# Unread matmuls ahead of two stretches of a transformer kernel, and its step lists reordered

## What is computed

```python
x = x + ln(phazor_conv(ln(x)))        # decaying complex filter along the tokens, real part
x = x + ln(moe8_top2(ln(x)))          # 8 experts of width 64, top 2, and a shared expert of 128
x = x + ln(attention(ln(x)))          # 16 heads of 64, l2-normed q and k, alibi, causal, 2 null keys
x = x + ln(moe4_top2(ln(x)))          # 4 unlike experts: swiglu 512, folded MLP, a two-norm block, MLP 512
```

## Time and profile before

| | before |
|---|---|
| median of the three runs | 1136.36 us |
| the profiled execution | 1135.25 us |
| its span, first to last instruction | 1133.5 us |
| PE / DVE / POOL / ACT busy | 90 / 69 / 51 / 49 % of the span |
| mean granted TensorE clock | 0.963 of full speed |

### The profile page before, as it was taken

The page is one execution under the profiler, slowest core; times in us unless marked ns, Lnnn a source line. Parts: engine busy times, 40 slices in busy tenths (PEclk is TensorE's granted clock), DMA queues, the critical chain, the costliest instruction groups (busy, mean ns, idle before and its releaser), DMA issues.

```text
span 1133.5 us, 18951 instructions
## 1 busy us (share of the span) xinstructions
...
## 2 busy tenths in 40 slices
...
DMA packets 21869, 11.29 MB, mean 10 GB/s; under 512 B 7440, under 2 KB 21136, under 8 KB 21648
## 3 DMA queue, kind: packets, MB, share of 16 engines
...
## 4 chain that ended last, share of the span: by engine, by line
PE 55%; DVE 24%; POOL 11%; issue 7%; ACT 2%; ACTq 0%; DVEq 0%; POOLq 0%
PE bank L1839 10%; POOL rnorm L835 7%; PE bank L1615 7%; PE bank L1841 4%; PE bank L1608 4%; PE bank L1609 3%; PE bank L1610 3%; PE bank L1739 3%; PE bank L1959 3%; PE bank L1965 3%; PE bank L1918 2%; PE bank L1799 2%; DVE sumsq L1435 2%; PE bank L1805 1%; PE bank L1869 1%
## 5 line engine op out<-in xcount | busy, mean ns | idle before, releaser
L835 POOL TENSOR_TENSOR rnorm<-sumsq,minus_half 128x16 f32<-128x16 f32 x64 | 187.7, 2949 | 21.6 <-DVE sumsq L1438 21.4
L843 POOL TENSOR_TENSOR unit<-unit,causal 128x256 f32<-128x256 f32 x128 | 89.7, 732 | 109.0 <-ACT unit L1062 109.0
L843 POOL TENSOR_TENSOR square<-square,causal 128x256 f32<-128x256 f32 x128 | 90.5, 737 | 101.4 <-ACT square L1062 101.4
L1799 PE MATMUL bank<-qT,kT 64*128 64x256 f32 x512 | 96.6, 389 | 0.0
L1462 DVE TENSOR_TENSOR denom<-bank,null_sum 128x4 f32<-128x4 f32 x128 | 20.3, 158 | 105.5 <-PE bank L1841 105.5
L1068 ACT ACTIVATE qT<-bank 128x512 f32<-128x512 f32 x64 | 38.4, 601 | 109.7 <-PE bank L1615 109.6
L1444 DVE TENSOR_TENSOR unit<-unit,rnorm 128x1024 f32<-128x1024 f32 x64 | 78.9, 1240 | 12.6 <-POOL rnorm L835 12.4
L1615 PEld LDWEIGHTS bank<-ident,unit 128*128 128x128 f32 x520 | 62.8, 150 | 33.3 <-issue 15.5
L1435 DVE TENSOR_REDUCE sumsq<-square 128x16 f32<-128x1024 f32 x64 | 77.7, 1214 | 11.6 <-ACT square L1024 11.3
L1615 PE MATMUL bank<-ident,unit 128*128 128x128 f32 x520 | 73.3, 289 | 13.5 <-DVE unit L1444 10.2
L1839 PE MATMUL bank<-val,unit 128*128 128x128 f32 x512 | 81.7, 282 | 4.2 <-DVE mixed L1466 4.0
...
## 6 DMA issues: line engine op xcount, KB each, us to landing
...
```

The source lines that it names most:

```text
L835: pool.tensor_tensor(rnorm[:, k, t, :], sumsq[:, t % 2, k, :], minus_half[:], ALU.pow).then_inc(a_root.sem, 1)
L843: m = pool.tensor_tensor(pd, pd, causal[:].unsqueeze(1).to_broadcast([P, 2, P]), ALU.mult)
L1799: return mm(bank[s][:, 2 * P * b:2 * P * (b + 1)], kT[rs, c, 2 * P * b:2 * P * b + P], qT[rs, c, 2 * P * b:2 * P * (b + 1)], start=True, s ...
```

## The change

Twenty matmuls are added in the set-up in four lots of five (`s_warm.0` to `s_warm.3`) and sixteen ahead of the last group's `f_turn`, in two lots of eight (`f_warm.0`, `f_warm.1`). Each multiplies 128x128 by 128x512 of weights that are in place and writes bank 6; nobody reads that result, and the next step that uses the bank writes over it. Three of the set-up lots and one of the last wait for a count of norm steps. Three of them stand between `s_turn` and `l_turn3`, and one between `l_turn3` and `l_route`.

All lists of all four engines are reordered. None loses or gains another step.

```diff
 PROLOGUE = {
     "PE": """
-e_turn1 l_turn2 s_turn l_turn3 l_route s_fold1 l_g.0 s_fold2 l_cT l_u.0 s_fold3 l_c.0 s_fold4 l_g.1 l_c.1 l_u.1
+e_turn1 l_turn2 s_turn s_warm.0 s_warm.1 s_warm.2 l_turn3 s_warm.3 l_route l_g.0 s_fold1 s_fold2 l_cT l_u.0 s_fold3
+l_c.0 s_fold4 l_g.1 l_u.1 l_g.2 l_c.1 l_u.2 l_g.3 l_u.3 l_c.2 l_g.4 l_u.4 l_c.3 E_turn1 l_down.0 l_down.1 l_down.2
...
     "DVE": """
-s_phase s_gain e_stats s_shift s_decay e_apply s_conv s_last e_scan e_sum s_w0 l_turn2 s_scale l_res s_raw l_norm
-l_turn3 s_pad l_route l_pick l_coef l_hg.0 s_v2 l_cT E_stats s_kvlo l_hu.0 l_hc.0 E_apply s_bias l_hg.1 l_hu.1 s_qlo
+e_stats s_phase s_gain s_shift s_decay e_apply s_conv s_last s_w0 e_scan e_sum l_turn2 s_scale s_raw l_res l_norm
+l_turn3 l_route s_pad l_pick s_v2 l_coef l_cT E_stats l_hg.0 s_kvlo l_hu.0 l_hc.0 E_apply s_bias l_hg.1 s_qlo l_hu.1
...
     "POOL": """
-e_stats s_sel s_slopes e_scan s_fill l_turn2 s_scale l_res s_colb E_stats E_scan l_dstats.0 l_dstats.1 l_astats.0
+e_stats s_sel s_slopes e_scan s_fill s_scale l_turn2 s_colb l_res E_stats E_scan l_dstats.0 l_dstats.1 l_astats.0
...
 FIRST = {
     "DVE": """
-a_mix.15 l_dstats.0 l_end.0 l_dstats.1 l_astats.0 l_end.1 l_aapply.0 l_xl.0 l_astats.1 a_o.0 e_sum l_aapply.1 a_o.1
-a_end.0 a_end.1 l_xl.1
+l_hc.1 a_mix.7 l_hu.2 a_mix.8 a_mix.9 l_hc.2 a_mix.10 l_hu.3 a_mix.11 l_hg.4 a_mix.12 l_hc.3 l_hu.4 e_sum a_mix.13
+a_mix.14 a_mix.15 l_dstats.0 l_dstats.1 l_end.0 l_astats.0 l_end.1 l_aapply.0 l_astats.1 l_xl.0 a_o.0 l_aapply.1
...
 MIDDLE = {
     "DVE": """
-f_out.3 a_mix.0 f_end_stats e_stats a_mix.1 l_hu.0 l_coef l_hg.1 a_mix.2 e_apply a_mix.3 l_hu.1 e_scan a_mix.4
-l_hg.2 l_cT l_hc.0 a_mix.5 l_hu.2 a_mix.6 l_hc.1 a_mix.7 l_hg.3 a_mix.8 a_mix.9 a_mix.10 l_hu.3 f_end a_mix.11
-l_hc.2 l_hg.4 a_mix.12 l_hu.4 l_hc.3 a_mix.13 e_sum a_mix.14 l_dstats.0 a_mix.15 l_end.0 l_dstats.1 l_astats.0
-l_aapply.0 l_end.1 l_astats.1 a_o.0 a_end.0 l_aapply.1 l_xl.0 a_o.1 l_xl.1 a_end.1
+l_coef f_out.3 a_mix.0 f_end_stats l_hu.0 a_mix.1 l_hg.1 e_stats a_mix.2 e_apply a_mix.3 e_scan l_hu.1 a_mix.4 l_cT
+l_hg.2 a_mix.5 a_mix.6 l_hc.0 l_hc.1 a_mix.7 l_hu.2 a_mix.8 l_hg.3 l_hc.2 a_mix.9 a_mix.10 l_hu.3 a_mix.11 l_hc.3
+l_hg.4 a_mix.12 l_hu.4 a_mix.13 e_sum a_mix.14 f_end a_mix.15 l_dstats.0 l_end.0 l_dstats.1 l_astats.0 l_aapply.0
+l_end.1 l_xl.0 l_astats.1 a_o.0 l_aapply.1 a_end.0 a_o.1 l_xl.1 a_end.1
     "POOL": """
-f_stats.0 f_stats.1 a_ss.0.0 a_ss.0.1 f_ce a_ss.1.0 a_keep f_ce_apply a_ss.1.1 a_ss.2.0 a_ss.2.1 f_ce2 l_turn2
-a_ss.3.0 a_ss.3.1 l_res f_bias a_scores.0 a_scores.1 e_stats a_scores.2 a_scores.3 a_scores.4 e_scan a_scores.5
-f_end_stats a_scores.6 a_scores.7 l_dstats.0 l_dstats.1 l_astats.0 l_astats.1 a_o.0 a_o.1
+f_stats.0 f_stats.1 a_ss.0.0 a_ss.0.1 f_ce a_ss.1.0 a_ss.1.1 f_ce_apply a_ss.2.0 a_ss.2.1 f_ce2 l_turn2 a_ss.3.0
+a_ss.3.1 l_res f_bias a_scores.0 a_scores.1 e_stats f_end_stats a_scores.2 a_keep a_scores.3 a_scores.4 e_scan
+a_scores.5 a_scores.6 a_scores.7 l_dstats.0 l_astats.0 l_dstats.1 l_astats.1 a_o.0 a_o.1
...
 LAST_A = {
     "DVE": """
-a_o.0 a_o.1 a_end.0 a_end.1
+a_mix.15 a_o.0 a_end.0 a_o.1 a_end.1
...
 LAST_F = {
     "PE": """
-f_turn.0 f_turn.1 f_ce.0 f_ce.1 f_sw.0 f_me.0 f_me.1 f_sw.1 f_ml.0 f_ml.1 f_ceT f_sw.2 f_relu.0 f_ml.2 f_relu.1
+f_warm.0 f_warm.1 f_turn.0 f_turn.1 f_ce.0 f_ce.1 f_me.0 f_me.1 f_sw.0 f_ml.0 f_sw.1 f_ceT f_ml.1 f_sw.2 f_relu.0
...
+            def warm(count, w):
+
+                for _ in range(count):
+                    mm(bank[6][:], w[:, 0:P], w[:, 0:N], start=True, stop=True)
+
+            def s_warm(k):
+                if k == 0:
+                    pe.wait_ge(w0_rounded, 2)
+                    pe.wait_ge(n_y.steps.sem, n_y.steps.at(0, 9))
+                elif k == 1:
+                    pe.wait_ge(n_y.steps.sem, n_y.steps.at(0, 13))
+                elif k == 2:
+                    pe.wait_ge(n_l.steps.sem, n_l.steps.at(0, 9))
+                warm(5, w0_gate.hi)
+
+            def f_warm(g, k):
+                if k:
+                    pe.wait_ge(n_o.steps[1].sem, n_o.steps[1].at(g, 5))
+                warm(8, w_kv.hi)
```

More of the change, by code:

```diff
@@ L58 @@
     "PE": """
[L59 to L63, removed]
+a_m.0 a_m.1 a_null a_t.0 a_m.2 a_v.0 l_turn2 a_t.1 a_m.3 a_v.1 a_t.2 l_turn3 a_t.3 a_v.2 a_v.3 l_g.0 a_scores.0
@@ L67 @@
[L67 to L71 removed]
+a_ss.0.0 a_ss.0.1 a_u.0.0 a_ss.1.0 a_null a_u.0.1 a_ss.1.1 a_u.1.0 a_ss.2.0 a_u.1.1 a_ss.2.1 a_u.2.0 l_turn2
@@ L72 @@
+a_ss.3.0 l_res a_ss.3.1 a_u.2.1 l_norm a_u.3.0 a_u.3.1 l_turn3 a_nexp l_hg.0 l_route l_pick l_hu.0 a_mix.0 l_coef
+e_stats a_mix.1 l_hg.1 a_mix.2 e_apply l_hg.2 a_mix.3 e_scan a_mix.4 l_hu.1 l_cT a_mix.5 l_hc.0 l_hg.3 a_mix.6
+l_hc.1 a_mix.7 l_hu.2 a_mix.8 a_mix.9 l_hc.2 a_mix.10 l_hu.3 a_mix.11 l_hg.4 a_mix.12 l_hc.3 l_hu.4 e_sum a_mix.13
+a_mix.14 a_mix.15 l_dstats.0 l_dstats.1 l_end.0 l_astats.0 l_end.1 l_aapply.0 l_astats.1 l_xl.0 a_o.0 l_aapply.1
+a_o.1 a_end.0 l_xl.1 a_end.1
 """,
     "ACT": """
-a_m.0 a_m.1 a_t.0 a_m.2 a_v.0 a_t.1 a_m.3 a_v.1 a_t.2 l_turn3 a_t.3 a_nexp a_v.2 a_v.3 l_g.0 a_scores.0 a_scores.1
@@ L107 @@
-a_nexp l_g.0 a_scores.1 l_g.1 l_g.2 a_scores.2 a_oT.0 a_scores.3 l_cT a_scores.4 a_oT.1 a_oT.2 l_g.3 a_scores.5
-a_scores.6 a_oT.3 l_g.4 a_oT.4 a_scores.7 a_oT.5 a_oT.6 a_oT.7 a_oT.8 l_x.0 l_x.1
+a_m.0 a_m.1 f_turn.0 f_turn.1 f_sw.0 a_t.0 f_me.0 f_sw.1 f_ceT a_m.2 f_relu.0 a_v.0 f_sw.2 f_relu.1 a_t.1 a_m.3
+f_sw.3 a_v.1 f_me.1 f_ml.0 f_ml.1 a_t.2 f_pick f_ml.2 f_ce2T a_t.3 a_v.2 f_ml.3 l_turn3 a_nexp a_v.3 a_scores.0
+l_g.0 l_exp a_scores.1 l_g.1 l_g.2 a_scores.2 a_oT.0 a_scores.3 a_oT.1 l_cT a_scores.4 a_oT.2 a_scores.5 l_g.3
@@ L118 @@
     "PE": """
[L119 to L124, removed]
+a_m.0 a_null a_m.1 f_turn.0 f_turn.1 f_ce.0 f_ce.1 f_sw.0 f_me.0 l_turn2 a_t.0 f_sw.1 f_ceT f_relu.0 a_m.2 f_relu.1
+f_sw.2 a_v.0 f_ce2 a_t.1 a_m.3 f_sw.3 a_v.1 f_ce2T f_me.1 a_t.2 f_ml.0 f_ml.1 f_ml.2 a_t.3 a_v.2 f_ml.3 a_v.3
+f_out.0 l_turn3 f_out.1 l_route a_scores.0 f_out.2 f_out.3 a_mix.0 a_scores.1 a_mix.1 l_g.0 l_u.0 a_mix.2 a_scores.2
+l_g.1 l_cT a_mix.3 a_oT.0 l_u.1 a_scores.3 a_mix.4 l_g.2 a_oT.1 a_mix.5 a_scores.4 a_mix.6 l_g.3 a_oT.2 a_mix.7
+l_u.2 a_scores.5 l_c.0 a_oT.3 a_mix.8 l_c.1 l_u.3 a_mix.9 l_g.4 l_c.2 a_oT.4 a_mix.10 a_scores.6 a_mix.11 l_c.3
+l_u.4 a_mix.12 a_scores.7 a_mix.13 l_down.0 a_oT.5 a_mix.14 l_down.1 a_mix.15 a_oT.6 l_down.2 a_oT.7 a_oT.8 l_down.3
 a_out.0 a_out.1 l_x.0 l_x.1
@@ L127 @@
     "DVE": """
[L128 to L132, removed]
@@ L133 @@
-a_mix.12 l_hu.4 a_mix.13 a_mix.14 l_dstats.0 a_mix.15 f_end l_dstats.1 l_end.0 l_astats.0 l_end.1 l_astats.1 a_o.0
-a_end.0 l_aapply.1 l_aapply.0 a_o.1 l_xl.0 a_end.1 l_xl.1
+f_stats.0 a_ss.0.0 f_stats.1 a_ss.0.1 f_apply.1 a_null f_apply.0 a_ss.1.0 a_u.0.0 f_route f_ce a_u.0.1 f_hid.0
+f_ce_apply a_ss.1.1 f_hid.1 a_u.1.0 a_u.1.1 a_ss.2.0 f_hid.2 a_ss.2.1 f_ce2 a_u.2.0 l_turn2 f_ce2_apply a_ss.3.0
+a_u.2.1 a_ss.3.1 f_hid.3 a_u.3.0 f_pick a_u.3.1 l_res l_norm l_turn3 l_route l_pick f_out.0 a_nexp f_out.1 a_mix.0
@@ L135 @@
+f_out.2 a_mix.1 l_hg.0 l_coef f_out.3 a_mix.2 l_hu.0 f_end_stats l_cT a_mix.3 l_hg.1 a_mix.4 l_hg.2 a_mix.5 a_mix.6
+l_hu.1 a_mix.7 l_hg.3 l_hu.2 l_hc.0 a_mix.8 l_hc.1 a_mix.9 l_hu.3 l_hc.2 a_mix.10 l_hg.4 a_mix.11 a_mix.12 l_hc.3
+l_hu.4 a_mix.13 a_mix.14 a_mix.15 l_dstats.0 l_end.0 l_dstats.1 f_end l_end.1 l_astats.0 l_astats.1 a_o.0 l_aapply.0
+l_aapply.1 a_o.1 l_xl.0 l_xl.1 a_end.0 a_end.1
 """,
     "ACT": """
-a_m.0 a_m.1 f_turn.0 f_turn.1 f_pick f_sw.0 a_t.0 f_sw.1 f_ceT f_me.0 f_relu.0 a_m.2 f_relu.1 f_sw.2 a_v.0 a_t.1
@@ L138 @@
-a_m.3 a_v.1 f_sw.3 a_t.2 f_me.1 f_ml.0 f_ce2T f_ml.1 a_t.3 a_v.2 f_ml.2 f_ml.3 a_v.3 l_turn3 a_nexp a_scores.0
-a_scores.1 l_exp l_g.0 a_scores.2 a_oT.0 l_g.1 a_scores.3 l_cT a_oT.1 l_g.2 a_scores.4 a_oT.2 a_oT.3 a_scores.5
-l_g.3 a_oT.4 a_scores.6 l_g.4 a_scores.7 a_oT.5 a_oT.6 a_oT.7 a_oT.8 l_x.0 l_x.1
+a_m.0 a_m.1 f_turn.0 f_turn.1 f_sw.0 a_t.0 f_sw.1 f_ceT f_me.0 f_relu.0 a_m.2 f_sw.2 f_relu.1 a_v.0 a_t.1 a_m.3
+f_pick f_sw.3 a_v.1 a_t.2 f_ml.0 f_me.1 f_ml.1 f_ce2T a_t.3 a_v.2 f_ml.2 f_ml.3 a_v.3 l_turn3 a_nexp a_scores.0
@@ L146 @@
+l_turn2 l_res f_bias a_scores.0 a_scores.1 a_scores.2 a_scores.3 a_scores.4 a_scores.5 a_scores.6 a_scores.7
+l_dstats.0 a_keep l_dstats.1 f_end_stats l_astats.0 l_astats.1 a_o.1 a_o.0
 """,
```

83 lines of the change are left out of this document (43 added, 40 removed).

## The result

The changed kernel took 1150.11 us (median of four runs, 1147.97 to 1152.21) against 1135.57 of the kernel before measured beside it (four runs, 1132.16 to 1138.4): ratio 1.0129, 95% interval 1.0095 to 1.0164. It is slower by 1.3%. I had forecast 1128.5 us, with 1122 to 1139 as the range.

What follows compares the result with a forecast made beforehand. PE was taken as the bound, busy 122.9 of 130 us in a middle stretch. Gains 1.2 + 0.5 + 3.0 + 2.0 + 0.3 + 0.8 = 7.8 us off 1135.25 gave 1127.5 profiled, 1128.5 median; range 1122 to 1139.

Steps and rivals of the forecast that it cites:

- the last sentence of the middle's POOL part: POOL, middle groups: f_ce_apply one root later only brings an earlier root forward; no time was counted for it.
- The rival on the slow side: DVE between heads 14 and 15, middle groups: late f_end holds up the experts' norm, 1145.5 us; chance 13%.
- a_keep: POOL, middle groups: moved behind a lot of masks, covered by PE's head work; 0.6 us in each of five, 3.0 gained.
- The other middle moves on DVE: Middle groups: e_stats, l_coef, the scan and f_end moved to shorten PE's waits; 0.4 us a group, 2.0 gained.
- Set-up and first group: Set-up: earlier s_turn and added matmuls raise the clock, 1.2 us gained; first group: e_sum moved to the heads, 0.5.
- The `FIRST` list: First group, DVE: e_sum leaves the norms between experts and attention for the heads; 0.5 us gained, 1.4 at best.
- The clock does not follow: Set-up and end: PE's clock stays low, set-up loses 1.0 us and the end gains nothing; 1131.5 us, chance 15%.
- The end: Last feed-forward: added matmuls could keep PE's clock up for 2.2 us; it would mostly fall again, so 0.8 taken.
- Only the ends count: Middle groups: one step's saved wait may be had by the next, leaving 2.8 us gained; 1133.6 us, chance 24%.

Runs made afterwards that it cites:

- end_back: root_undone with f_end put back in its old place behind l_hu.3 in DVE's middle list: 1131.10 us, ratio 0.9958.
- keep_alone: The kernel before with only a_keep moved, from between the roots of q and k to behind the third lot of masks: ratio 0.9959.
- root_undone: The changed kernel with the root of a_ss.1.1 behind f_ce_apply again in POOL's middle list, a_keep staying in its new place: ratio 0.9966.
- middle_keep: The changed kernel with the four middle lists as before and only a_keep moved in them: ratio 0.9936.
- pool_back: The changed kernel with POOL's whole middle list as before: 1134.28 us, ratio 0.9989.
- middle_back: The changed kernel with all four engines' middle lists as before: 1134.19 us, ratio 0.9998.
- no_s_warm: middle_keep without the 20 unread matmuls of the set-up: 1130.26 us, ratio 0.9947.
- the exchange: In POOL's middle list the root of a_ss.1.1 goes ahead of f_ce_apply; made alone on the kernel before: 1150.76 us, ratio 1.0132.

## Why the prediction was wrong

**The step that failed** is the last sentence of the middle's POOL part: "Moving `f_ce_apply` one root later only brings an earlier root forward." I priced it at nothing and named no cover for it. It costs 15 us, alone. The root of `a_ss.1.1` did come forward, from 8.9 to 6.0 us behind the start of the `n_c` root, but POOL had to stand 0.66 us for its sum of squares and then met DVE's product (0.92 us). What counts is the end of the last root, since DVE waits for that, and it came 1.6 us later; PE's longer wait at `f_ml` then brought the clock down. The rows for this stood in the trace of before, in the timelines of POOL and DVE between 604 and 620 us. I had read that DVE waits for the last root and that its row is unbroken from there to `f_ml`, and had used this for `a_keep` only.

**The rival on the slow side** had the wrong place. `f_end` did not hold up the experts' norm: no new wait at `l_x`, and `end_back` changes nothing. That the range ended at 1139 was due to it: no case held a new wait ahead of `f_ml`.

**`a_keep`**: right in place and sign. 3.0 us forecast, 4.7 measured with `keep_alone`; the row that I had named gives 2.8 of it (five times 0.55).

**The other middle moves on DVE**: 2.0 us gained by my term. `root_undone` against `middle_keep` says 0.3% lost, but the intervals touch, and `pool_back` against `middle_back`, which differ in these moves too, says 0.1% gained. So no gain is shown. The waits moved rather than went: in the five stretches the scan's (2.1 us) and that for `l_hg` (3.6) are gone in `root_undone`, but there are 4.1 for `l_hu`, 3.1 instead of 0.7 for `f_turn`'s input and 10.9 instead of 2.6 for `a_u` (each against `middle_keep`); all of PE's waits there sum to 41.4 us against 36.5.

**Set-up and first group**: `l_turn3` at 39.96 where I said 39.5, transposes 0.60 as forecast, `l_route` 0.4 us sooner than before instead of 0.9. At 45.89 PE waits 0.95 us for ACT's copy of the folded weights, a cover that I had not named. Some 0.5 us of lead are left at the last fold (L1672 before, L1693 now), 53.95 against 54.46, but the clock falls there at 54.1 (55.2 before), the row takes 3.51 us instead of 2.93, and `l_g.1` starts at 57.40 against 57.32. The `FIRST` list, 0.5 us gained by my term, is 1.7 us late by the mark of the changed kernel; by the runs its cost can't be told from nothing.

**The clock does not follow**: wrong, the clock followed at both ends. Rows of `no_s_warm` speak again of transposes: up to 38.64 PE had done nothing but transposes, the granted clock rose at 35.8, and the four of `l_turn3` took 0.66 us, not 1.06. This speaks against the page that I had weighed, by which transposes do not count as PE being busy in the way matmuls do (the Trainium skill, TensorE: Matmul & The Clock Gate, Part 4: PE-mode transpose). The end kept its clock, which I had valued at 0.8 of 2.2 us; the profiled end is 2.1 us shorter, yet the runs with and without those matmuls are equal within 0.2%. What the profile shows for one execution is not what the median gained.

**Only the ends count**: ends alone 0.9990; with `a_keep` and the new `LAST` lists 0.9928. So a gain of the size that was forecast (0.7%) can be had from parts of this change; the exchange costs nearly twice that.
